# Output projection of the first four row tiles moved between the two attention passes, with seven rounds of top-k beside it; the index weights' loads split in two kinds

## The reference

```python
q = (rmsnorm(xn @ q_a_w) @ q_b_w)            # 32 heads of 128 + 64 (rope)
kv = rmsnorm(ckv[..., :64]) @ kv_b_w         # keys and values from a latent of 64
iq, ik = xn @ idx_wq_w, xn @ idx_wk_w        # index: 16 heads of 128
idx = einsum(iw, relu(iq . ik)), causal      # [1024, 1024]
mask = top_k(idx, 128) & causal              # per query row
attn = softmax(where(mask, scores, -inf))    # 32 heads
x + (attn @ v) @ o_w + experts(xn)           # out: [1024, 512]
```

## Time and profile before

| | us |
|---|---|
| median of three runs (range) | 872.99 (871.05 to 873.15) |
| the profiled execution | 871.49 |
| its span | 869.7 |
| index stage of tiles 7 and 6 | 187.8 to 269.9 |
| low pass | 269.4 to some 481 |
| high pass | some 481 to 773.9 |
| last stage | 773.9 to 869.7 |

### The profile page before, as it was taken

How to read it: one execution, slowest core, us unless ns; L and a number is a source line. 1 busy time by engine, 2 the same in 40 slices (tenths; PEclk the granted TensorE clock), 3 DMA queues, 4 the chain that set the end, 5 groups by cost and what they waited for, 6 DMA issues and landing times.

```text
span 869.7 us, 20144 instructions
## 1 busy us (share of the span) xinstructions
PE 789.4 (91%) x7432; PEld 488.3 (56%) x7432; DVE 658.7 (76%) x1558; ACT 587.7 (68%) x1325; POOL 559.8 (64%) x478
## 2 busy tenths in 40 slices
PE   5999989977777989888987999999999999999998
PEld 2555544434444555555554667767777776764443
DVE  6367678899999999999997888888888888851000
ACT  3687889978886888878886776666776766740000
POOL 3177478877885676676676788888878888640000
PEclk9999999999999999999999999999999999999999
DMA  8022211203334555556654576887678888861110
GB/s 262 25 73 75 60 49 49 80 14 105 110 100 121 140 150 153 149 142 152 150 152 125 98 161 139 152 155 150 128 137 162 135 153 150 174 135 49 49 49 24
DMA packets 185697, 100.85 MB, mean 116 GB/s; under 512 B 133632, under 2 KB 159616, under 8 KB 185600
## 3 DMA queue, kind: packets, MB, share of 16 engines
q1 hardware_dynamic: 185600, 99.57, 49.7%
HBM read 36.62 MB, written 6.29 MB: 49 GB/s over the span
## 4 chain that ended last, share of the span: by engine, by line
POOL 32%; PE 24%; issue 14%; DVE 13%; DMA 8%; SPq 7%; ACT 3%; POOLq 0%; DVEq 0%; ACTq 0%
PE psS L804 10%; DMA arena<-arena 7%; SPq L478 5%; POOL arena L1543 4%; POOL arena L1541 4%; DVE m L1234 4%; POOL arena L1548 4%; PE psT L602 4%; POOL arena L1570 3%; POOL ikT L1570 3%; PE psS L615 3%; PE psT L582 2%; DVE bias L1241 2%; POOL bias L1518 2%; SPq L425 2%
## 5 line engine op out<-in xcount | busy, mean ns | idle before, releaser
L731 PE MATMUL psS<-keyT,arena 128*128 128x512 f16 (+3 forms) x1152 | 229.7, 327 | 7.4 <-DVE small L1299 3.9
L835 ACT ACTIVATE arena<-psT 128x512 f16<-128x512 f32 (+3 forms) x344 | 162.1, 503 | 103.0 <-PE psT L788 64.5
L1299 DVE CUSTOM_DVE_ANT_0 arena<-psS,bias 128x512 f32<-128x512 f32 (+7 forms) x256 | 191.2, 750 | 36.1 <-PE psS L731 15.7
L1026 ACT ACTIVATE arena<-arena,small 128x512 f32<-128x512 f32 (+7 forms) x256 | 197.5, 774 | 28.8 <-DVE small L1299 23.6
L1077 DVE SCALAR_TENSOR_TENSOR arena<-psT,arena 128x512 f16<-128x512 f32 (+3 forms) x262 | 135.1, 536 | 24.4 <-ACT arena L835 24.0
L731 PEld LDWEIGHTS psS<-keyT,arena 128*128 128x128 f16 x1152 | 91.7, 98 | 71.5 <-issue 12.7
L615 PE MATMUL psS<-ikT,big 128*128 128x512 f16 (+3 forms) x528 | 103.2, 340 | 24.1 <-DVE bias L1167 20.6
L788 PE MATMUL psT<-ident,arena 128*128 128x128 f32 x672 | 105.5, 278 | 17.2 <-DVE arena L1077 9.3
L1518 POOL TENSOR_TENSOR bias<-arena,bias 128x768 f32<-128x768 f32 (+2 forms) x48 | 91.4, 1920 | 33.1 <-ACT arena L905 22.3
L788 PEld LDWEIGHTS psT<-ident,arena 128*128 128x128 f32 x672 | 77.4, 141 | 45.3 <-ACT arena L1026 29.2
L615 PEld LDWEIGHTS psS<-ikT,big 128*128 128x128 f16 x528 | 49.3, 100 | 73.1 <-DVE bias L1167 28.5
(11 more groups left out here) (165 smaller groups left out, 1403.4 us busy)
## 6 DMA issues: line engine op xcount, KB each, us to landing
arena<-arena SPq DMA_DIRECT2D x192, 128.0 KB, 2.4
arena<-in_wiq SPq DMA_DIRECT2D x32, 256.0 KB, 2.8
arena<-in_ow SPq DMA_DIRECT2D x16, 512.0 KB, 3.8
arena<-in_qbT SPq DMA_DIRECT2D x16, 256.0 KB, 2.5
wvo_parts<-arena SPq DMA_DIRECT2D x16, 256.0 KB, 2.3
arena<-in_qpe SPq DMA_DIRECT2D x16, 128.0 KB, 3.0
arena<-in_x SPq DMA_DIRECT2D x8, 256.0 KB, 3.0
out<-arena SPq DMA_DIRECT2D x8, 256.0 KB, 2.0
```

The lines of the kernel that those rows point to most:

```text
L731: last = mm(bank[:, k:k + w], Q[:, u % 2, h, a, q:q + P], keyT[:, b, h, k:k + w], start=(a, b) == (0, 0), stop=(a, b) == (1, 0))
L835: return nc.scalar.activation(dst, src, ACT.Copy, scale=scale)
L1026: nc.scalar.activation(pr_of(g)[:, 0:kw], pr_of(g)[:, 0:kw], ACT.Exp, bias=shift[:, g % 8:g % 8 + 1], scale=-1.0, accum_out=rsum[:, unit_o ...
L1299: v.tensor_tensor_reduce(out=pr_of(g)[:, 0:kw], in0=bank[:, 0:kw], in1=bias[:, TOFF[t]:TOFF[t + 1]], scale=-c_s, scalar=3e38, op0=ALU.add, ...
```

## The change

1. **Four tiles of the last stage move.** At the end of step 127 PE runs `middle()`: `products` and `experts` for tiles 0 to 3, in four half banks, with the last values and the last transposition of the low pass between them. The scores of steps 128 to 130 leave steps 125 to 127 and stand at the end of `middle()`. The parts come from sixteen places (`mid_at`); fifteen are loaded from DRAM (`load_mid`) ahead of it, one is still in `vo_s`. Tiles 4 to 7 stay in the last stage, each in its own half bank; tiles 4 to 6 leave out part 15 first and take it up at the end.
2. **Marks move.** The index loop of tiles 7 and 6 keeps 48 marks of tiles 5 and 4 (two or four for each head, none for the last). The other 16 and two masks go to the low pass, with 36 marks of tiles 7 and 6. The last 28 marks (seven rounds) and two masks of tiles 7 and 6 stand in DVE's `middle()`.
3. **Loads in two kinds.** `load_qw` (two DMAs, now waiting for `qw_mm` alone and issued one head earlier) and `load_pe` (one DMA, on its own semaphore `ld_pe`).
4. **First scores.** Scores 0 and 1 no longer wait for the last addition of tile 6; score 2 does. DVE no longer waits for masks 4 and 5 there.
5. **`store_vo`** of unit u - 1 moves from its step 7 to step 0 of unit u, behind the four `place` DMAs.
6. Input rows are loaded into a buffer of their own (`rows_out`) in both passes; tiles 0 to 3 are stored after step 140.

```diff
+        EARLY_MARKS, LATE_MARKS = 2 * 24, 28 + 2
+        STEP_MARKS = MARKS[0][EARLY_MARKS:] + MARKS[1][:len(MARKS[1]) - LATE_MARKS]
+        for mark_ in STEP_MARKS:
+            MARK_STEPS.setdefault(so_far_ * (LOW - 4) // weight_, []).append(mark_)
+            so_far_ += mark_[0] + 1
@@ sync
+            def load_pe(p):
+                u = p % 2
+                if p >= 2:
+                    sp.wait_ge(pe_lo, 2 * p - 2)
                 sp.dma_start(pe_s[:, u]..., qpe[:, :, ds(2 * p, 2), :]).then_inc(ld_pe[u], 16)
...
                 if s == 0 and 2 <= u + 1 < NU:
                     place(u + 1, latent, qa_lo, q_lat, 1)
                     place(u + 1, turned, q_rot, q_tur, 0)
+                if s == 0 and 0 < u <= NP:
+                    store_vo(u - 1)
                 if s and turns(g):
                     turn(g)
...
-                if s == 7 and u < NP:
-                    store_vo(u)
...
+                if g == LOW - 1:
+                    sp.wait_ge(*landing(DMA_LOW - 1))
+                    sp.wait_ge(av_mm, summed(BY_DMA[DMA_LOW - 1]))
+                    sp.wait_ge(vo_lo, NP)
+                    sp.wait_ge(max_done, LOW)
+                    load_mid(3)
@@ tensor
+            def middle():
+                pe.wait_ge(max_done, LOW)
+                for k in range(NP - MID_HELD):
+                    arrived(k)
+                    for t in range(3):
+                        mid_products(t, k)
+                    if k < len(LOW_LAST):
+                        values(LOW_LAST[k])
+                    if k == MID_LAG - 2:
+                        wait_freed(BEFORE[LOW_OUT])
+                        out_T(psT[BANK[LOW_OUT]], NP - 1)
+                    if k >= MID_LAG:
+                        mid_products(3, k - MID_LAG)
...
+                scores(LOW)
...
+                scores(LOW + 1)
...
+                experts(mid_bank[3], 3)
+                scores(LOW + 2)
@@ scalar
-                act.wait_ge(qw_mm, n + 1)
                 u = n % 2
+                act.wait_ge(ld_pe[u], 16 * (n // 2) + 16)
                 copy(w1hi[:, n, 0:128], pe_s[:, u, 0, :], WQ_S).then_inc(qw_hi, 1)
                 copy(w2s[:, n, 0:128], pe_s[:, u, 1, :], WQ_S).then_inc(qw_hi, 1)
+                act.wait_ge(qw_mm, n + 1)
@@ vector
-                top_round(GROUPS[1])
+                for mark in MARKS[0][early(n):early(n + 1)]:
+                    top_part(*mark)
...
+            def middle():
+                for mark in late[:4]:
+                    top_part(*mark)
+                unit_out(NP - 1)
+                for mark in late[4:12]:
+                    top_part(*mark)
+                ot_low(psT[BANK[LOW_OUT]], NP - 1)
+                for mark in late[12:]:
+                    top_part(*mark)
+                for t in range(2):
+                    final(half_bank[t], t)
@@ gpsimd
                 elif d - DMA_LOW == 0:
...
+                    pool.wait_ge(fin_mm, NT // 2)
```

More of the change, by code:

```diff
@@ L296, in due, with due_in_loop @@
             return [g for g in range(max(0, x - max(LAGS)), min(x, STEPS)) if g + lag(g) == x]
+        LOW = 8 * NP
+        LOW_LAST = [g_ for x_ in range(LOW, LOW + LAGS[0]) for g_ in due(x_) if g_ < LOW]
+        def due_in_loop(x):
+            return [g for g in due(x) if x < LOW or g >= LOW]
         AV_AT = {}
@@ L301, in block_kernel @@
                 AV_AT[g_] = len(AV_AT)
+        assert sorted(LOW_LAST) == list(range(LOW - len(LOW_LAST), LOW)) and max(AV_AT[g_] for g_ in LOW_LAST) == LOW - 1
         def ri_before(u):
@@ L776, in _, with products, experts @@
             pe.wait_ge(raw_done, 2)
+            def products(bank, t, n, parts, first):
+                for a, b in ((0, 0), (0, 1), (1, 0)):
+                    mm(bank, big[:, a, n, ds(t * P, P)], parts[n][:, b, :], start=first and (a, b) == (0, 0), stop=False)
+            def experts(bank, t):
+                for a, b in ((0, 0), (0, 1), (1, 0)):
+                    last = mm(bank, hwT[:, a, ds(t * P, P)], bmp[:, b, :], start=False, stop=(a, b) == (1, 0))
+                last.then_inc(fin_mm, 1)
@@ new lines, in _, with mid_products, arrived @@
+            mid_bank = half_bank[0:3] + (psO[:],)
+            def mid_products(t, k):
+                products(mid_bank[t], t, MID[k], mid_at, k == 0)
+            def arrived(k):
+                for j in range(4):
+                    if MID[k] == min(MID_GROUP[j], key=MID.index):
+                        pe.wait_ge(ld_mid[j], 16 * len(MID_GROUP[j]))
+                if MID[k] == NP - 2:
+                    pe.wait_ge(ot_lo, NP - 1)
+                if MID[k] == NP - 1:
+                    pe.wait_ge(ot_lo, NP)
+                    pe.wait_ge(vo_lo, NP)
@@ L796, in _ @@
                         q_job(bank[:], what, at)
-                for late in due(g):
+                for late in due_in_loop(g):
                     values(late)
-            def products(t, u, pairs):
-                for n in pairs:
-                    for a, b in ((0, 0), (0, 1), (1, 0)):
-                        mm(psS[u][:, 0:CH], big[:, a, n, ds(t * P, P)], wvo[n][:, b, :],
-                           start=n == 0 and (a, b) == (0, 0), stop=False)
-            def experts(t, u):
-                for a, b in ((0, 0), (0, 1), (1, 0)):
-                    last = mm(psS[u][:, 0:CH], hwT[:, a, ds(t * P, P)], bmp[:, b, :], start=False, stop=(a, b) == (1, 0))
-                last.then_inc(fin_mm, 1)
-            pe.wait_ge(ld_vo, 16 * NP)
+                if g == LOW - 1:
+                    middle()
+            pe.wait_ge(ld_vo, 16 * (NP - 2))
             pe.wait_ge(max_done, STEPS)
-            products(0, 0, range(NP))
-            experts(0, 0)
+            for n in range(NP - 1):
+                if n == NP - 2:
+                    pe.wait_ge(ot_lo, NU - 1)
+                products(half_bank[0], 4, n, wvo, n == 0)
             for g in range(STEPS, STEPS + LAGS[1]):
@@ L1061, in _ @@
                     rope_hi(unit_of(g) + 2)
+                if g == LOW - 1:
+                    ot_evac(psT[BANK[LOW_OUT]], NP - 1)
+                    for e in range(LOW, LOW + AHEAD - 1):
+                        exp_step(e)
             ot_evac(psT[0], NU - 1)
```

257 lines of the change are left out of this document (156 added, 101 removed).

## The result

The changed kernel took 881.78 us in the median of four runs (881.08 to 883.76), the kernel before 873.07 beside it (871.05 to 873.45): a ratio of 1.0109, 95% interval 1.0093 to 1.0125. It is 1.1% slower. I had forecast 869.8 us and faster. The time lies just inside the range (852 to 882), the sign is wrong, and what happened is the second rival, the stores that land late (880 us).

A forecast was written before the change was run, and what follows sets the result against it. DVE was taken to bound the index stage and, closely followed by PE and ACT, the low pass; PE the high pass. Terms -8.4, -1.0, +10.2, -1.5, -2.0 and +0.3 gave -2.4 us: 869.8 us, range 852 to 882.

The forecast's parts named there:

- the second rival: Low pass: stores land late; at 3.0 us ACT waits 1.71 us in 15 units, sum +8.1, 880 us; chance 0.2.
- index loop: Index stage of tiles 7 and 6: fewer marks shorten DVE's heads until ACT's path decides, -8.4 us.
- last addition to first maximum: Between index stage and low pass: masks go, two copies stay, scores 0 and 1 are ready, -1.0 us.
- 14 units (forecast: 15): Low pass: ACT's waits for the store, +15.2 us, less 5.0 for DVE's marks, make +10.2 us.
- fifteenth `rope_hi` to the end of the high pass, less 44.1: Between the passes PE's waits for scores go, -1.5 us; stores and row loads in the high pass, +0.3.
- last stage, plus 44.1: Last stage: PE's wait for a free bank goes with four banks, -2.0 us; moved tiles give nothing in the sum.
- The failed step: Low pass: the moved store lands 2.3 us after issue, so ACT stands still 1.01 us in each of 15 units.
- the term of the store: Low pass: ACT's V copy waits for the moved store, 1.01 us in each of 15 units, +15.2 us.
- The marks' 5.0 us: Low pass: fewer marks in steps 4 and 5 shorten DVE's part up to the next `rope_hi`, -5.0 us in all.
- DVE's cover in `middle()`: Between the passes: DVE's 35.4 us fit within PE's 38.4, covered by 3 us, so marks there cost nothing.
- The third rival: Index stage gives 3 us only, because ACT can't work ahead: sum +3, 874.5 us; chance 0.15.
- The first rival: Low pass: the store is in time, POOL bounds units at 12.1 us, -9.5; sum -22, 849 us; chance 0.2.

The follow-up runs named there:

- kernel 11: The change with its store back in step 7, plus the rope swap issued in step 1 ahead of the transposition: 849.83 us, 0.974 of before.
- kernel 6: The changed kernel with the store put later still, in step 3 behind the transposition and ahead of the rope swap: 912.04 us, 1.047 of before.
- kernel 10: The changed kernel with SP issuing a low unit's transpositions only once that unit's store has landed: 878.09 us, 1.006 of before.
- kernel 3: The changed kernel with the store between the two latent and the two turned place DMAs: 853.98 us, 0.979 of before.
- kernel 2: The kernel before with only the store moved, to step 0 of the next unit behind the four place DMAs: 898.43 us, 1.029 of before.
- kernel 9: The change with its store back in step 7, plus the 28 last marks in the low pass instead of between the passes: 864.59 us, 0.990 of before.
- kernel 5: The changed kernel with its store cut into two 128 KB DMAs, ACT's copy waiting for the high half only: 864.97 us, 0.992 of before.
- kernel 8: The change with its store back in step 7, plus 32 instead of 48 marks left in the index loop: 851.60 us, 0.976 of before.

## Why the prediction was wrong

Measured are differences of the two profiled executions; in the last column kernel 1, the change without its move of the store.

| stretch | forecast | changed | kernel 1 |
|---|---|---|---|
| index loop | -8.4 | -9.0 | -9.0 |
| last addition to first maximum | -1.0 | -1.0 | -1.0 |
| first maximum to first `rope_hi` | | -0.5 | -0.5 |
| 14 units (forecast: 15) | +10.2 | +23.9 | -5.4 |
| fifteenth `rope_hi` to the end of the high pass, less 44.1 | -1.2 | +0.9 | -2.2 |
| last stage, plus 44.1 | -2.0 | -2.2 | -2.2 |
| sum | -2.4 | +12.2 | -20.3 |

The fifth row takes the stretch between the passes (-1.5) and the high pass (+0.3) together, since the same work stands on both sides of their boundary.

**The failed step is one factor of one term.** "The store follows 0.04 later and lands 2.3 later (median of 16)". The order of waits was right, and so was the issue: 3.04 forecast, 3.05 measured. But 2.3 us is the median of stores in step 7, where nothing follows for 1.1 us. Behind the change a transposition is issued 0.7 us behind the store's start. The landing was 3.0, the copy 0.75 us later than forecast, and 15 x 0.75 = 11.3 us of the 14.6 by which the sum was missed. So the term of the store was 26.4 us (15 x 1.76) where I had 15.2. The rival had it word for word ("at 3.0 ... 880"), and the earlier trace rows with their maximum of 4.0 showed that the median was not a property of the store. A term that is 15 times a landing also wants its mean, and that was 2.5 us in the trace of before, with which the sum would have been about zero. (The sum turns positive at 2.46, not at 2.6 as I wrote; and the 849 and 874.5 of two rivals were counted from 871.5 us, the 869.8 and 880 from 872.2.) The landings measured, with their company:

| where | issued ahead, behind | median us |
|---|---|---|
| before, step 7 | nothing ahead, four DMAs 1.1 us behind | 2.3 |
| kernel 1, step 7 | the same | 2.0 |
| kernel 11, step 7 | a load 3.5 us ahead still landing, four DMAs 1.1 us behind | 3.2 |
| kernel 6 | transposition ahead, swap behind | 2.3 |
| kernel 10 | four DMAs ahead, nothing behind | 2.4 |
| kernel 3 | two ahead, two behind | 2.5 |
| changed, kernel 2 | four ahead, transposition behind | 3.0 |

That what is issued behind the store, the transposition first of all, makes 0.6 of it is shown by kernel 10; that the DMAs ahead make the other 0.4 is only read off the table.

The first two rows have the same neighbours on SP's list, the third nearly so, and still they differ. The profile shows one more thing in flight, single packets of 16 KB on a queue called `instruction`. Two stores of before, the first issued at 450.81, the second at 348.53:

```profile
q8 instruction: 1, 0.02, 1.4%
...
wvo_parts<-arena SPq DMA_DIRECT2D x1, 256.0 KB, 4.0
```

```profile
q1 hardware_dynamic: 144, 0.26, 35.2%
...
wvo_parts<-arena SPq DMA_DIRECT2D x1, 256.0 KB, 2.0
```

In before, ten of the 16 stores had such a packet under way later than 0.6 us after their issue, and these ten landed in 2.1 to 4.0 us; the other six landed in 2.0. In kernel 1 the seven with one took 2.1 to 3.6 and the nine without 2.0; in kernel 11 the eleven with one took 2.2 to 4.5. It isn't all: in kernel 11 three of the five without one took 2.9 to 4.3, and in kernel 9 two stores with one took 2.0. In the changed kernel none of the 16 stores met one. So the spread of the earlier trace rows goes with these packets in before and kernel 1, and the 3.0 of the change is another matter, the neighbours on SP's list; no run changed when the packets come.

**The marks' 5.0 us.** They came back in kernel 1: from the DVE copy that waits for ACT (called T below; 2.08 us behind the V copy) to the next `rope_hi` 6.00 us instead of 6.32 (the unit, less the V copy's place in it, less 2.08), 15 x 0.32 = 4.8. In the changed kernel it was 6.24. Here the clock has a part. Three units of after, with PE's granted clock behind the busy times:

```profile
320.10:334.30 14.20, 12.19 (x115) 7.78 (x114) 10.89 (x33) 10.59 (x32) 8.92 (x8) 0.88 0.52 137
348.90:363.20 14.30, 11.86 (x124) 7.44 (x122) 12.05 (x36) 10.59 (x32) 8.93 (x8) 1.00 0.51 130
392.90:407.80 14.90, 12.68 (x119) 7.80 (x118) 10.98 (x33) 10.49 (x33) 8.95 (x8) 0.89 0.57 146
```

Each unit has a clock of 1.00 or of 0.88 to 0.89 (a mean over its time at 2.4 and at 1.2 GHz). The seven at 1.00 took 6.00 us from T to the next `rope_hi`, kernel 1 in the same seven 5.89; the seven lower ones 6.48, kernel 1 there 6.11. So some 2.6 us (7 x 0.37) go with the clock; before and kernel 1 stand at 1.00 in all 14 units. How such a stretch looks, at the end of the low pass:

```profile
486.09 0.90 PE L905 MATMUL psT<-ident,arena 128*128 128x128 f32 x3 [2.33 <-ACT arena L1138]
486.79 0.63 PE L704 MATMUL psT<-qlT,w1hi 128*128 128x512 f16 x1
487.21 0.63 PE L705 MATMUL psT<-qlT,w1hi 128*128 128x512 f16 x1
...
490.79 0.44 PE L905 MATMUL psT<-ident,arena 128*128 128x128 f32 x2 [0.82 <-ACT arena L1138]
```

After an idle time of 2.33 us PE's matmuls start 0.42 us apart (486.79, 487.21) instead of 0.216. It came with the waits, and no run took the clock away alone. Kernel 5 comes nearest: it still waits for the store in each of 15 units, 19.5 us in all instead of 31.6, its clock is 1.00 over the 14 units, and from T to the next `rope_hi` it takes 5.9 us.

```profile
275.34:461.92 186.58, 158.55 (x1653) 99.82 (x1651) 156.95 (x460) 146.26 (x423) 125.31 (x112) 1.00 0.60 154
```

**Between the passes and in the high pass** I had -1.2. Kernel 1 has -2.2; the changed kernel has +0.9, of which 1.8 is the fifteenth unit's own wait for the store. PE's waits for the scores went, and two for ACT took their place: 2.0 us in kernel 1, where I had counted some 2.4, and 3.15 (2.33 and 0.82 above) in the changed kernel. DVE's cover in `middle()` was 2.2 us where I had 3: its two additions end at 527.65, and PE comes to scores 128 only at 529.81, without a wait. DVE, and then PE:

```profile
526.37 1.28 DVE L1483 SCALAR_TENSOR_TENSOR rows_out<-psS,rows_out 128x512 f32<-128x512 f32 x2
531.44 1.23 DVE L1430 CUSTOM_DVE_ANT_0 arena<-psS,bias 128x1024 f32<-128x1024 f32 x1 [3.79 <-PE psS L791]
```

```profile
529.81 1.46 PE L791 MATMUL psS<-keyT,arena 128*128 128x512 f16 x6
```

**The index loop** and **the last stage** came out as reckoned; a head of two marks takes 3.49 to 3.96 us from addition to addition, where I had 3.50, and 1.8 us more in all for waits. The third rival (ACT can't work ahead, -3) is out for 48 marks; kernel 8, in which 16 marks less gave only 2.3 us, suggests that it is just behind. The first rival (849) had the size of what the rest of the change is worth; its reason, POOL's ring at 12.1, was wrong, as kernel 11 and the unit of 12.39 show, so that its closeness is luck.

**The weighing** was poor: I gave the late landing 0.2 and slower 0.3 in all, although each 0.17 us of it moved the sum by 2.6 and the place had changed from a quiet one to a crowded one. With a landing anywhere between 2.3 and 3.0 the sum lay between -2.4 and +8.1, and slower began at +3.4: slower deserved nearly half.

## What to carry to other kernels

A DMA's landing time belongs to what is under way beside it, not to the DMA: when it is moved, look at what is issued within a microsecond ahead of it and behind it, and take the slow end of the row if that gets fuller. Where a buffer is reused by the engine that a chain hangs on, its store has to be issued early enough to have landed by then, or it needs a second buffer (which gave back 23 of the 30.6 us); here one store in the wrong place cost 30.6 us in 15 units. And a change of many parts is measured with its parts apart: this one hid a gain of 2.5% behind a net loss of 1.1%.

## What the runs showed of the hardware

The same 256 KB store landed in 2.0 to 3.0 us (medians) by its neighbours on the queue, and a transposition behind it cost more than one ahead of it (2.4 to 3.0, against 2.3). In step 7 of before and kernel 1 it landed in 2.0 us alone and in 2.1 to 4.0 when a 16 KB packet of the queue `instruction` was under way. Its own issue row on SP went from 0.33 us in step 7 to 0.59 behind other DMAs. And the waits seem to cost twice: in seven of 14 units PE's granted clock fell to 0.88 or 0.89, and the rest of those units was some 0.37 us longer than in kernel 1, while the other seven, with waits of the same kind, kept 1.00 and were 0.11 longer.
